# Attention of a fused four-layer kernel: one masking addition for the two heads of a diagonal step

## What is computed

```
scores = einsum('bhid,bhjd->bhij', q, k) * scale          # 16 heads of 32, sequence 2048
scores = scores + alibi_causal_bias(s, NUM_HEADS)         # -inf where j > i
attn = softmax(scores, axis=-1)
out = einsum('bhij,bhjd->bhid', attn, v)
```

## Time and profile before

| | us |
|---|---|
| median of 3 runs | 1642.31 |
| lowest and highest run | 1640.88, 1651.42 |
| the profiled execution | 1642.89 |
| its span in the trace | 1641.1 |

### The profile page before, as it was taken

One profiled execution on the slowest core, in us unless ns is written; L12 is line 12 of the kernel. 1 busy time (PEld: TensorE's weight loads), 2 busy tenths in 40 slices (PEclk: granted clock), 3 DMA queues, 4 the chain that ended last, 5 costly groups with the idle time before them and its releaser, 6 DMA issues. The chain is left out here.

```text
span 1641.1 us, 22085 instructions
## 1 busy us (share of the span) xinstructions
PE 1542.0 (94%) x7906; PEld 1076.4 (66%) x7906; DVE 999.8 (61%) x1719; ACT 593.5 (36%) x1125; POOL 641.7 (39%) x534
## 2 busy tenths in 40 slices
PE   5999989999999999997988999969999998999998
PEld 4887545454545545543667888857777776888887
DVE  7774887887878788873545655555464455232332
ACT  3121245555545555555212222254423231222221
POOL 4100277858868786700327677633020201000000
PEclk9999799999999999999899999989999999999999
DMA  6877544544526464301762222163030231420210
GB/s 237 248 256 202 128 132 117 118 108 141 121 63 171 119 135 99 108 15 33 247 215 65 65 77 72 46 204 113 1 129 1 78 93 50 148 103 1 103 52 26
DMA packets 104443, 182.07 MB, mean 111 GB/s; under 512 B 28712, under 2 KB 45224, under 8 KB 103684
## 3 DMA queue, kind: packets, MB, share of 16 engines
q1 hardware_dynamic: 87176, 119.20, 25.2%
q0 software_dynamic: 13520, 53.85, 11.1%
q10 hardware_dynamic: 3640, 7.61, 1.3%
HBM read 118.62 MB, written 61.74 MB: 110 GB/s over the span
## 5 line engine op out<-in xcount | busy, mean ns | idle before, releaser
L1072 ACT ACTIVATE att_probs<-att_ring 128x512 f32<-128x512 f32 (+3 forms) x640 | 298.2, 536 | 283.5 <-DVE att_ring L1103 145.8
L1094 DVE TENSOR_REDUCE att_maxes<-att_ring 128x2 f32<-128x1024 f32 (+7 forms) x366 | 339.2, 948 | 66.3 <-PE att_ring L992 55.4
L1025 PE MATMUL att_outp<-att_probs,att_vs 128*64 128x512 f32 (+3 forms) x1280 | 271.1, 545 | 0.4 <-ACT att_att L1056 0.4
L1025 PEld LDWEIGHTS att_outp<-att_probs,att_vs 128*64 128x64 f32 x1280 | 78.3, 137 | 120.0 <-issue 68.8
L1804 DVE TENSOR_TENSOR glu_hid<-glu_sig,glu_u 128x512 f32<-128x512 f32 x44 | 30.3, 688 | 140.6 <-PE glu_u L1744 140.6
L1013 PE MATMUL att_ring<-route_wah,route_wbh 102*128 102x512 f32 (+2 forms) x320 | 105.4, 403 | 6.4 <-DVE att_maxes L1094 5.2
L992 PE MATMUL att_ring<-route_wbh,route_wah 100*128 100x512 f32 (+2 forms) x320 | 102.8, 405 | 6.9 <-DVE att_maxes L1094 4.4
L1013 PE MATMUL att_ring<-moew_wal,moew_wbl 102*128 102x512 f32 (+2 forms) x320 | 101.1, 398 | 5.2 <-DVE att_maxes L1094 5.1
L992 PE MATMUL att_ring<-moew_wbl,moew_wal 100*128 100x512 f32 (+2 forms) x320 | 96.6, 378 | 3.8 <-DVE att_maxes L1094 2.3
L1013 PEld LDWEIGHTS att_ring<-route_wah,route_wbh 102*128 102x128 f32 x320 | 54.9, 191 | 68.6 <-issue 39.1
L2413 POOL TENSOR_TENSOR lin_sig<-lin_o_copy,lin_sig 128x512 f32<-128x512 f32 x16 | 20.4, 1277 | 198.5 <-ACT lin_o_copy L2266 198.5
(11 more groups left out here) (294 smaller groups left out, 3451.0 us busy)
## 6 DMA issues: line engine op xcount, KB each, us to landing
att_q_raw<-in_w POOLq DMA_DIRECT2D x48, 352.0 KB, 4.0
w_ternary<-att_q_out POOLq DMA_DIRECT2D x24, 352.0 KB, 2.7
tail_up<-w_ternary SPq DMA_DIRECT2D x22, 256.0 KB, 4.6
xn<-qkv_x SPq DMA_DIRECT2D x4, 1024.0 KB, 7.4
q_hi<-qkv_hi SPq DMA_DIRECT2D x16, 256.0 KB, 3.7
q_lo<-qkv_lo SPq DMA_DIRECT2D x16, 256.0 KB, 4.5
k_hi<-qkv_hi SPq DMA_DIRECT2D x16, 256.0 KB, 2.9
k_lo<-qkv_lo SPq DMA_DIRECT2D x16, 256.0 KB, 3.9
```

Source lines behind the costliest of these rows:

```text
L1025: last = pe.matmul(outp[v_cols(h), off:CH], vs[p % 2][:, kt, v_cols(h)], probs[:, g % 4, h, off:CH], start=kt == 0, stop=kt == TT * (c + 1 ...
L1072: act.activation(probs[:, g % 4, h, off:CH], ring[:, rg.banks["score", g][h], off:CH], ACT.Exp).then_inc(exped, 1)
L1094: last = dve.tensor_reduce(maxes[:, hs, t, g:g + 1], banks[:, :, 0:width], AX.X, ALU.max)
```

## The change

Where the two banks of a diagonal step are neighbours, VectorE waits for both heads' scores and masks both blocks in one addition over 128 x 2 x 128, and raises `masked` by 2 when it is done. For the 18 diagonal steps with banks 0 and 6 nothing changes. Beside that, before the two small products of the expert routing (`ranks` and `places`) TensorE waits until both banks of their pair are free, not only the first.

```diff
                     if g == RANKS_AT:
-                        wait_freed(("ranks", 0), 0)
+                        for h in range(2):
+                            wait_freed(("ranks", 0), h)
                         router.ranks(pe)
                     if g == PLACES_AT:
-                        wait_freed(("places", 0), 0)
+                        for h in range(2):
+                            wait_freed(("places", 0), h)
                         router.sum_places(pe)
...
                 off, _ = main_span(*MAIN[g % NS])
+                low, high = rg.banks["score", g]
+                if high == low + 1:
+                    block = ring[:, low:high + 1, off:off + P]
+                    dve.wait_ge(scored, 2 * g + 2)
+                    dve.tensor_tensor(block, block, over_heads(neg_k, slice(0, 2)), ALU.add).then_inc(masked, 2)
+                    return
                 for i, h in enumerate(rg.heads(("score", g))):
```

## The result

| | before | after |
|---|---|---|
| median of 20 runs each, us | 1644.74 | 1655.43 |
| lowest and highest | 1640.55, 1651.42 | 1650.38, 1663.94 |
| ratio (95% interval) | | 1.0070 (1.0057 to 1.0082) |
| the profiled execution, us | 1642.89 | 1654.92 |
| its span, us | 1641.1 | 1653.1 |

The change costs 1.0070 x 1644.74 - 1644.74 = 11.5 us, with an interval of 9.4 to 13.5; the two medians by themselves lie 10.7 us apart. I had worked out 6.3. The direction was right, the size was about half. Against the first three runs I had said 1649 us.

What follows compares the result with a forecast made beforehand. The prediction took TensorE to bound the kernel, with VectorE having room. Its terms, 4.4 + 1.1 + 0.5 + 1.4 + 0.4 - 1.0 - 0.5 = +6.3 us on 1642.9, gave 1649.2, stated as 1649 us, range 1643 to 1656.

Steps and rivals of the forecast that it cites:

- TensorE bound, VectorE with room; the path to the second unit without slack: Attention stage: TensorE sets the pace, VectorE is 80% busy; each 0.12 us of later mask costs TensorE 0.12 us.
- The first head's mask comes 0.13 us later, the start 0.25 or 0.12: Even diagonal steps: longer addition +0.13 us, later start +0.25 us with 512 columns a head or +0.12 with 256.
- Raising `masked` by 2, taken at 0: Semaphore update on the merged addition: goes with the instruction as before, 0, at most some hundredths each way.
- Three matmuls: Even diagonal steps: score, mask, exponential and the second unit's matmul must follow within TensorE's time for three matmuls.
- Where it is paid: Diagonal steps over 8 head pairs: losses of 4.4, 1.1, 0.5, 1.4 and 0.4 us, gains of 1.0 and 0.5.
- I take 0, with 3.0 as the bound: Places 10 and 22: 3.0 us of delay, taken as 0 because TensorE waits for VectorE's maxima within four steps.
- Rival C: Diagonal steps: nothing absorbs the delay, so slower by more, +13.4 us or 1656.3, range 1653 to 1662; chance 0.17.
- Place 36, late in three head pairs: Place 36: three pairs pay 1.1 us together; three where VectorE is already late pay only 0.5 us together.
- Places 0 and 2, odd steps: Places 0 and 2: +0.4 us, bound 3.0; odd diagonal steps: 0, bound 3.6 us.
- The gains of 1.5 us: TensorE gains 1.0 us at the 14 waits of places 14 and 26, and 0.5 us on the first 12 steps.
- The router's waits: hidden: Waits before the routing products: hidden behind older waits for VectorE results; without that cover under 1 us, twice.

Runs made afterwards that it cites:

- start_only: Kernel before, but the first of the two additions waits for both scores where the banks are neighbours; 1649.14 us, ratio 1.0024.
- release_only: Kernel before, but ScalarE waits for both masks before the first exponential where the banks are neighbours; 1653.94 us, ratio 1.0051.
- quiet_after: Changed kernel with GpSimd's ternary-weight arithmetic cut to 8 of 704 columns, all but the first piece; 1645.16 us.
- quiet_before: Kernel before with GpSimd's ternary-weight arithmetic cut to 8 of 704 columns, all but the first piece; 1633.13 us.
- router_waits: Kernel before with only the change's two waits before the routing products; 1645.61 us, ratio 0.9998.
- odd_merged: Changed kernel with the merged addition on odd diagonal steps alone; 1643.37 us, ratio 0.9998 to the kernel before.
- changed_again: The changed kernel as it is, run again for a second profile; 1659.01 us, ratio 1.0075 to the kernel before.
- even_merged: Changed kernel with the merged addition on even diagonal steps alone; 1657.48 us, ratio 1.0069 to the kernel before.
- half_block: Changed kernel with its merged addition cut to the first 64 of each head's 128 columns; one run, 1643.84 us.

## Why the prediction was right and wrong, point by point

*TensorE bound, VectorE with room; the path to the second unit without slack.* Right. The three timelines of before in which VectorE came late gave the slope of 1, and start_only and release_only confirm it: 0.24 us later is 0.24 us longer.

*The first head's mask comes 0.13 us later, the start 0.25 or 0.12.* The two parts are right to 0.01 us (start_only: +0.24 and +0.12). What is missing is 0.07 us between the wait, now an instruction of its own, and the addition. The sum per pair is 0.24 + 0.13 + 0.07 = 0.44 where I had 0.37, and 0.12 + 0.13 + 0.07 = 0.32 where I had 0.25. Over the 36 pairs at places 8, 10, 20, 22, 36 and 38 that pay this makes 2.5 us. The units of the trace of before could not have told me, since the same form starts there without the 0.07.

*Raising `masked` by 2, taken at 0.* This is the first step that failed: I had put it at nothing, "with no more than some hundredths each way", and looked only at the update, not at the wait that goes with it. The addition that raises by 2 has its wait in front of it, and that is the 0.07 us above (that the one brings about the other is the link not shown).

*Three matmuls.* The text of the prediction gives the path the time "in which TensorE makes three matmuls". Three products are meant, which is two matmuls each; the readings from the rows don't depend on it.

*Where it is paid.* This is the second step that failed, and the larger one. The quiet pair of kernels shows it with little chance in it. The sums over all head pairs, quiet_after less quiet_before, beside the predicted ones:

| places | predicted, us | measured, us |
|---|---|---|
| 8 and 20 | +4.4 | +5.3 |
| 36 | +1.6 | +2.6 |
| 38 | +1.4 | +1.7 |
| 10 and 22 | 0 | +3.9 |
| 0 and 2 | +0.4 | -0.3 |
| 12 and 14 | -0.5 | -1.5 |
| sum | +7.3 | +11.7 |

The predicted column lacks the two gains that can't be seen in this pair: 0.5 us at place 26, and 0.5 on the first steps, where the clock and the cast make the head pair 0 differ by 1 to 2 us from profile to profile. For that reason places 6 and 16 of head pair 0, 2.2 us longer in quiet_after, are not in the table, and places 0, 2 and 14 of head pair 0 are, with 1.1 us that are shorter by the same chance. One pair at place 26 is left out too: in quiet_before it took 7.02 us (4.02 in quiet_after), as TensorE's clock fell there.

"I take 0, with 3.0 as the bound" for places 10 and 22 was wrong. They pay in full, 0.31 to 0.33 us in each of 12 places, and places 12 and 14 give back 1.5 us in the quiet kernels (1.2 without head pair 0), all that the pair at place 14 had to give (3.99 down to 3.83 us). Place 26 gives nothing back there. So a stall does cover a delay, but only for as long as it lasts, and here it is shorter than the delay. With GpSimd at work the waits at places 14 and 26 are longer, and in principle could swallow more. Counted over 13 such pairs in each profile, with 3.83 us as the shortest at place 14 and 3.96 at place 26, the excess is 13.1, 13.6 and 12.4 us in before, router_waits and odd_merged, and 10.5, 9.0 and 11.8 in after, changed_again and even_merged. That is some 2.6 us given back of 3.9, but single pairs differ by 3 us from one profile to the next (start_only, release_only and half_block, with smaller delays, have 12.6, 9.9 and 6.8), so how much of a delay these stalls swallow stays open. The times don't settle it: had the stalls swallowed all of the 3.9, the change would cost some 2.5 us less than the 12.0 of the quiet pair, about 9.5, which the interval of 9.4 to 13.5 just holds. Rival C let places 10 and 22 pay, because "the stalls at place 14 move along with TensorE". In paying it was right and its sum of +13.4 nearer; the reason is another in the quiet pair, where the stall doesn't move along but is used up. Its other parts, odd steps and places 0 and 2, did not come.

*Place 36, late in three head pairs.* I priced them low because VectorE came late there in the one profile, and against that profile they did pay little (0.07, 0.20 and 0.32). But that lateness is itself chance: quiet_after less quiet_before, all six pay 0.40 to 0.44.

*Places 0 and 2, odd steps.* The sum for places 0 and 2 is right, but not the way to it: without head pair 0 they come to +0.5 us in the quiet pair where I had +0.4, and I had counted nothing for the merged mask of step 0. It costs 0.44 at place 0 in six head pairs, and -0.30 to -0.50 at place 2 takes most of it back, since TensorE has less to wait there. The odd steps are right: odd_merged loses nothing.

*The gains of 1.5 us.* At places 12 and 14 more came than I had said, but how much of it is gain and how much delay given back isn't told apart; at place 26 and in the first steps nothing that can be told from chance.

*The router's waits: hidden.* Right.

*The forecast.* Of the 4.4 us between the two sums, 3.9 are places 10 and 22 (0.8 of them the 0.07 us a place); 2.2 are places 8, 20, 36 and 38, where the 0.07 us a place (1.7) and the three that I had taken as late were missing; places 0 and 2 take 0.7 off again, and 12 and 14 take 1.0. The two gains of 0.5 us that I had also counted bring the predicted sum to 6.3; the measurement, 11.5, shows nothing of them.

*A rule.* The rule of the Trainium skill that I had weighed (Perfetto Trace Analysis, Optimizing Scalar/DVE Operations), that larger instructions help a saturated engine and smaller ones an engine that causes bubbles elsewhere, agrees with the direction: 7.8 us less in masks on VectorE, 11.5 us more time. It names the case, not the cause: in release_only both small additions stand as before, and 8.4 us are lost by when the first is passed on.

## What to carry to other kernels

An instruction that serves two consumers ends later for the first of them and starts only when the later of its inputs is there; here it also lost 0.07 us because its wait had become an instruction of its own. These three add up, and all of it is paid where a chain of engines has no slack. Before merging, find for each instance who reads the first half and when: here the odd steps could be merged at no loss (and no gain that the time shows), and the even ones cost the whole 11.5 us. And a stall further on covers a delay only for as long as the stall itself lasts, if it doesn't move along with the delay: at place 14 of the quiet kernels that was 0.16 us of 0.32, at place 2 it was 0.35 of 0.44.

## What the runs showed of the hardware beyond that

TensorE's granted clock can fall at a stall in mid-stage. In the profile after, at place 14 of one head pair, TensorE stood 1.34 us for maxima that a held cast (2.34 us) had made late; the clock fell at 666.6 us, 0.7 us after the end of that wait, and TensorE then stood another 1.23 us. Up to 664 us the granted clock was 1.00. The windows from there (start:end, length, busy us (instructions) of PE, PEld, DVE, ACT and POOL, granted clock, DMA share, GB/s):

```profile
664.00:668.00 4.00, 1.82 (x8) 0.85 (x5) 3.90 (x9) 2.47 (x5) 3.62 (x4) 0.83 0.05 18
668.00:673.00 5.00, 4.60 (x11) 1.60 (x11) 3.84 (x8) 0.60 (x1) 4.88 (x4) 0.50 0.46 146
```

```profile
669.98 3.65 PE L1025 MATMUL att_outp<-att_probs,att_vs 128*64 128x512 f32 x8
```

The clock goes from 2.4 to 1.2 GHz, and the eight matmuls of the sums take 3.65 us instead of 1.94. That pair of steps took 9.51 us in all, 4.21 before. Such a fall came once or twice or not at all per profile between 230 us and the end of the stage, in kernels with and without the change (none in before and odd_merged, two in router_waits), so it doesn't explain the difference. All ten falls in the thirteen profiles come at or close behind such waits of TensorE (1.44 us in quiet_before), but a wait of 1.40 us in before and one of 1.70 us in odd_merged had no fall behind them, so what else it takes the runs don't show. That it spreads the runs fits the 34 runs of the kernel before: the longer ones have the lower mean clock (correlation -0.69).

An order of TensorE that only puts one sum between a score and a unit made most steady pairs 0.22 to 0.45 us longer (4.15 for 3.88 us at place 8; those at place 2 became 0.3 us shorter) and the kernel 33 us slower. With the same matmuls, the added time of a pair off the diagonal (4.28 for 3.95 us) stands at the two more changes between kinds: the first matmul of the sums follows a score by 0.33 us, where a unit follows by 0.23, and the rest lies where the sums end and the unit begins. The cause of that is not shown.
